# Sandwich transformer layer on 8 cores: five x buffers, a V projection that takes its first four tiles in step, and V weights held back

## The reference

```python
q = (x @ w_q.T).reshape(B, S, H, Hd)      # likewise k, v
scores = jnp.einsum('bqhd,bkhd->bhqk', q, k) * scale
p = jax.nn.softmax(scores, axis=-1)
o = jnp.einsum('bhqk,bkhd->bqhd', p, v).reshape(B, S, D)
attn = o @ w_o.T
ffn = (silu(x @ w_gate.T) * (x @ w_up.T)) @ w_down.T   # hidden 8192

x = x + _layernorm(attn(_layernorm(x)))
x = x + _layernorm(ffn(_layernorm(x)))
```

## Time and profile before

| What | Value |
|---|---|
| Time, median of 3 runs | 2342.87 us (2342.86 to 2342.87) |
| Profiled execution, its own time | 2356.09 us |
| Its span, slowest core (core 4) | 2354.5 us |
| Spans of cores 0 to 7 | 2334.1, 2336.4, 2339.5, 2337.5, 2354.5, 2354.4, 2333.1, 2339.7 us |
| Mean granted TensorE clock, cores 0 to 7 | 0.994, 0.993, 0.992, 0.992, 0.980, 0.980, 0.993, 0.991 |
| TensorE busy, core 4 | 2285.1 us, 97% of the span |
| ACT, DVE, POOL busy, core 4 | 584.7, 575.4, 130.8 us |
| Chain that ended last | PE 90%, DVE 3%, ACT 2%, DMA 2%, issue 2% |
| Matmul of 128x512, from start to start at full clock | 215 ns; at half clock about 427 ns |

### The profile page before, as it was taken

One profiled execution on the slowest core, in us unless ns is written; L12 is line 12 of the kernel. 1 busy time (PEld: TensorE's weight loads), 2 busy tenths in 40 slices (PEclk: granted clock), 3 DMA queues, 4 the chain that ended last, 5 costly groups with the idle time before them and its releaser, 6 DMA issues.

```text
span 2354.5 us, 26957 instructions; the slowest of 8 cores (2333.1 to 2354.5 us)
## 1 busy us (share of the span) xinstructions
PE 2285.1 (97%) x10656; PEld 1034.9 (44%) x10656; DVE 575.4 (24%) x771; ACT 584.7 (25%) x781; POOL 130.8 (6%) x249
## 2 busy tenths in 40 slices
PE   4999999999999989999999999999999999999997
PEld 2444444444444434444444444444444444444443
DVE  4510034554554565510110110011001100000005
ACT  2421166666666642220000000000000000000003
POOL 1000000000000000000000000000000000000000
PEclk9999999999999988889999999999999999999999
DMA  9530021322323053154444444444444474435473
GB/s 229 156 59 14 9 36 28 63 37 35 56 36 63 10 125 135 72 99 74 79 75 78 76 77 77 76 77 75 79 74 80 73 131 75 77 67 87 75 179 143
DMA packets 43852, 186.34 MB, mean 79 GB/s; under 512 B 4816, under 2 KB 4816, under 8 KB 37584
## 3 DMA queue, kind: packets, MB, share of 16 engines
q0 software_dynamic: 36816, 134.27, 34.5%
q1 hardware_dynamic: 6912, 50.33, 6.1%
HBM read 302.06 MB, written 16.78 MB: 135 GB/s over the span
## 4 chain that ended last, share of the span: by engine, by line
PE 90%; DVE 3%; ACT 2%; DMA 2%; issue 2%; DVEq 0%; POOL 0%; ACTq 0%; SPq 0%; POOLq 0%
PE ps L162 90%; DMA wvs<-wv 1%; DMA xs<-xb 1%; DVE x L789 1%; ACT tt L165 0%; ACT pt L165 0%; ACT qt L168 0%; DVE rec L441 0%; DVE st L557 0%; DVE st L583 0%; ACT x L165 0%; ACT pvc L168 0%; ACT sdv L165 0%; ACT ln3t L168 0%; DVE fs L771 0%
## 5 line engine op out<-in xcount | busy, mean ns | idle before, releaser
L162 PE MATMUL ps<-ln3t,we 128*128 128x512 bf16 x4096 | 893.0, 381 | 0.8 <-ACT ln3t L168 0.8
L162 PEld LDWEIGHTS ps<-ln3t,we 128*128 128x128 bf16 x4096 | 402.4, 98 | 488.8 <-issue 25.8
L162 PE MATMUL ps<-ln1t,w 128*128 128x512 bf16 x1536 | 370.7, 379 | 3.0 <-ACT qt L168 3.0
L165 ACT ACTIVATE pt<-ps,kon 128x1024 bf16<-128x1024 f32 x256 | 284.7, 1114 | 191.8 <-PE ps L162 191.5
L165 ACT ACTIVATE sil<-ps 128x512 f32<-128x512 f32 x128 | 76.4, 597 | 789.5 <-PE ps L162 789.4
L162 PE MATMUL ps<-wvs,ln1t 128*128 128x512 bf16 x1024 | 227.1, 383 | 6.0 <-DMA wvs<-wv 6.0
L162 PEld LDWEIGHTS ps<-ln1t,w 128*128 128x128 bf16 x1536 | 148.2, 98 | 189.5 <-issue 14.7
L162 PE MATMUL ps<-ring,ga 128*128 128x512 bf16 x1024 | 222.1, 379 | 1.4 <-DVE gb L670 1.0
L162 PE MATMUL ps<-ring,gb 128*128 128x512 bf16 x1024 | 221.7, 379 | 0.0
L162 PEld LDWEIGHTS ps<-wvs,ln1t 128*128 128x128 bf16 x1024 | 100.4, 99 | 125.8 <-issue 10.7
L162 PE MATMUL ps<-pt,vt 128*128 128x512 bf16 x512 | 153.7, 382 | 0.7 <-ACT pvc L168 0.7
(11 more groups left out here) (50 smaller groups left out, 853.0 us busy)
## 6 DMA issues: line engine op xcount, KB each, us to landing
we<-wg POOLq DMA_DIRECT2D x64, 512.0 KB, 6.0
we<-wu POOLq DMA_DIRECT2D x64, 512.0 KB, 6.0
ring<-wd POOLq DMA_DIRECT2D x64, 512.0 KB, 6.1
xs<-xb SPq DMA_DIRECT2D x16, 1024.0 KB, 8.9
wvs<-wv POOLq DMA_DIRECT2D x16, 512.0 KB, 15.3
w<-wq POOLq DMA_DIRECT2D x16, 512.0 KB, 5.1
w<-wk POOLq DMA_DIRECT2D x16, 512.0 KB, 5.2
wo<-wo POOLq DMA_DIRECT2D x4, 2048.0 KB, 16.1
```

The source lines that it names most:

```text
L162: return op("t", lambda e: e.matmul(dst, lhsT, rhs, start=start, stop=stop), ctr)
L165: return op("s", lambda e: e.activation(dst, src, fn, bias=bias, scale=scale), ctr)
```

## The change

Six parts:

1. `xs` has five buffers in place of three. Two of them lie in the part of `vt` that group 3 of V fills later. The load of tile `tc` now waits for the normalisation of tile `tc - 5`; five loads go out at once.
2. Group 1 of V's weights and the first three Q and K weight tiles no longer follow group 0 at once: group 1's four chunks wait, one each, until x tiles 7, 9, 11 and 13 have landed, and the Q and K tiles until x tile 15 has.
3. `v_proj` is split by chunk into `v_part(tc, g, c)` (four matmuls) and `v_out` (the copy to `vt`). The first four tiles take group 0 in step: after the transposition of tile `tc`, the tiles before it take chunk `tc - 1`, then tile `tc` takes chunks 0 to `tc - 1`; chunk 3 follows for all four, then their four copies.
4. From tile 4 on the order is `v_proj(k, 0)`, `x_transpose(k + 1)`, and the next `k`.
5. Group 1 is projected after all of group 0; before, its tiles 0 to 11 stood between the tiles of group 0.
6. `x_norm_behind(tc)` puts the statistics of one tile ahead of the normalisation of the tile before it, as the old loop did.

```diff
-    XS = at("xs", OT_O, 6144, F32)
+    XS = [at("xs%d" % i, o, 2048, F32) for i, o in enumerate(
+        (OT_O, OT_O + 8192, OT_O + 16384, VT_O + 49152, VT_O + 57344))]
...
     def x_load(tc):
-        if tc >= 3:
-            wt("y", xnorm[tc - 3])
-        x_in[tc] = dma("y", XS.r((tc % 3) * 2048, 2048), xb[tc * 128:(tc + 1) * 128, :], dX[tc % 3])
+        if tc >= 5:
+            wt("y", xnorm[tc - 5])
+        x_in[tc] = dma("y", XS[tc % 5].r(0, 2048), xb[tc * 128:(tc + 1) * 128, :], dX[tc % 5])
...
-    def wv_load(g):
+    def wv_load(g, after=(None, None, None, None)):
+
         for c in range(4):
             if g >= 2:
                 wt("g", v_pe[(NTC - 1, g - 2)])
+            wt("g", after[c])
             wv_in[(g, c)] = dma("g", WV.r((g % 2) * 8192 + c * 2048, 2048), wv[g, c, :, :], dWV[g % 2][c])
 
     v_pe = {}
     v_sb = {}
-    v_n = [0]
-
-    def v_proj(tc, g):
-        b = 4 + v_n[0] % 4
-        v_n[0] += 1
-        wt("t", lnt[tc], bank_free[b])
-        for kc in range(NKC):
-            if kc % 4 == 0:
-                wt("t", wv_in[(g, kc // 4)])
+    v_bank = {}
+
+    def v_part(tc, g, c):
+
+        if c == 0:
+            v_bank[(tc, g)] = 4 + len(v_bank) % 4
+            wt("t", lnt[tc], bank_free[v_bank[(tc, g)]])
+        b = v_bank[(tc, g)]
+        wt("t", wv_in[(g, c)])
+        for kc in range(4 * c, 4 * c + 4):
             tok = mm(PS.r(b * 512, 512), LN1T.r(kc * 2048 + tc * 128, 128),
                      WV.r((g % 2) * 8192 + kc * 512, 512), kc == 0, kc == NKC - 1,
                      tV if kc == NKC - 1 else None)
-        v_pe[(tc, g)] = tok
-        wt("s", tok)
+        if c == 3:
+            v_pe[(tc, g)] = tok
+
+    def v_out(tc, g):
+        b = v_bank[(tc, g)]
+        wt("s", v_pe[(tc, g)])
         bank_free[b] = v_sb[g] = copy_s(VT.r(g * 8192 + tc * 512, 512), PS.r(b * 512, 512), sV)
+
+    def v_proj(tc, g):
+        for c in range(4):
+            v_part(tc, g, c)
+        v_out(tc, g)
...
-    for tc in range(3):
+    def x_norm_behind(tc):
+
+        if tc < NTC:
+            x_stats(tc)
+        x_norm(tc - 1)
+        if tc + 4 < NTC:
+            x_load(tc + 4)
+
+    for tc in range(5):
         x_load(tc)
     wv_load(0)
-    wv_load(1)
+    x_stats(0)
+
+    for tc in range(4):
+        x_norm_behind(tc + 1)
+        x_transpose(tc)
+        if tc:
+            for t in range(tc):
+                v_part(t, 0, tc - 1)
+            for c in range(tc):
+                v_part(tc, 0, c)
+    x_norm_behind(5)
+    for t in range(4):
+        v_part(t, 0, 3)
+    for t in range(4):
+        v_out(t, 0)
+    x_transpose(4)
+    for k in range(4, NTC):
+        if k + 2 <= NTC:
+            x_norm_behind(k + 2)
+        v_proj(k, 0)
+        if k + 1 < NTC:
+            x_transpose(k + 1)
+    wv_load(1, [x_in[tc] for tc in (7, 9, 11, 13)])
+    wt("g", x_in[NTC - 1])
     for m in range(3):
         w_load(m)
-    x_stats(0)
-    x_stats(1)
-    x_norm(0)
-    x_transpose(0)
-    x_load(3)
-    x_stats(2)
-    x_norm(1)
-    for k in range(NTC):
-        if k + 4 < NTC:
-            x_load(k + 4)
-        if k + 3 < NTC:
-            x_stats(k + 3)
-        if k + 2 < NTC:
-            x_norm_later = k + 2
-        else:
-            x_norm_later = None
-        if k == 0:
-            x_transpose(1)
-        if x_norm_later is not None:
-            x_norm(x_norm_later)
-        v_proj(k, 0)
-        if k + 2 < NTC:
-            x_transpose(k + 2)
-        if k >= 4:
-            v_proj(k - 4, 1)
-    wv_load(2)
-    for tc in range(12, NTC):
-        v_proj(tc, 1)
-    wv_load(3)
-    for g in (2, 3):
+    for g in (1, 2, 3):
+        if g >= 2:
+            wv_load(g)
         for tc in range(NTC):
```

More of the change, by code:

```diff
@@ L185, in build_nc @@
     NEGSH = KON.r(1, 1)
-    dX = [C("dX%d" % i) for i in range(3)]
+    dX = [C("dX%d" % i) for i in range(5)]
     dWV = [[C("dWV%d%d" % (i, c)) for c in range(4)] for i in range(2)]
@@ L222, in x_stats @@
     def x_stats(tc):
-        p, sl = tc % 2, tc % 3
+        p, xs = tc % 2, XS[tc % 5]
         wt("v", x_in[tc], aggr.get(tc - 2))
         for c in range(4):
-            op("v", lambda e, c=c: e.bn_stats(ST.r(p * 24 + c * 6, 6), XS.r(sl * 2048 + c * 512, 512)), vB)
+            op("v", lambda e, c=c: e.bn_stats(ST.r(p * 24 + c * 6, 6), xs.r(c * 512, 512)), vB)
         aggr[tc] = row_aggr(p)
     def x_norm(tc):
-        p, sl = tc % 2, tc % 3
+        p, xs = tc % 2, XS[tc % 5]
         row_rstd(p, aggr[tc])
@@ L234, in x_norm @@
         xnorm[tc] = op("v", lambda e: e.tensor_scalar(
-            XN.r(p * 2048, 2048), XS.r(sl * 2048, 2048), MV.r(p * 2, 1), SDV.r(p * 2 + 1, 1),
+            XN.r(p * 2048, 2048), xs.r(0, 2048), MV.r(p * 2, 1), SDV.r(p * 2 + 1, 1),
             ALU.subtract, ALU.mult), vXN)
```

## The result

| | Before | Changed |
|---|---|---|
| Median of 7 runs | 2342.87 us | 2356.57 us |
| Median of the undisturbed runs (7 and 4) | 2342.87 us | 2355.9 us |
| Ratio, with its 95% interval | | 1.0056 [1.0044, 1.0068] |
| Spans of the profiled cores | 2333.1 to 2354.5 us | 2349.6 to 2353.8 us |
| First Q projection, mean of 8 cores | 278.1 us (276.7 to 282.1) | 293.0 us (291.5 to 294.2) |

The change makes the kernel slower by 0.56%, 13.0 us; forecast were 12.4 us, 2355.3 us. On all eight cores the loss sits in the first stage: its end is 11.7 to 16.9 us later, 14.9 in the mean. In some executions part of the chip is granted a lower clock, whatever the kernel; the ratios leave out only the clearly slow ones, the counts and ranges of runs in the experiments all of them.

The account below looks back on a forecast made before the run. TensorE, 97% busy, was bound early by waits for data. Stage end 46.2 + 77.0 + 165.6 = 288.8 against 277.33, +11.5; clock +1.7, other cores -0.8: +12.4 on 2342.87 gives 2355.3 us, 8-in-10 range 2348.5 to 2366.

Parts of the forecast that it names:

- x and weights in pairs of 6.6 us: First stage's loads: an x tile and a weight chunk land together every 6.6 us, x3 at 25.5, x4 at 32.1.
- The early part: Tiles 0 to 3: tile 4's transposition starts at 46.2 with 64 matmuls done, won by about 6 us.
- The exposed latency: Tiles 4 to 15: each projection waits for its own tile's copies, 6.42 us for 4.35, 24.8 us of new waiting.
- The clock: TensorE in the new waits of about 2.0 us: one fall to the lower clock per core, 1.7 us.
- Stages after it, DVE, DMA, POOL cost nothing: Later stages unchanged and TensorE-bound; in the loop DVE's 5.2 us and DMA's 4.3 us fit within 6.42 us.
- The other cores: Other cores stood about 1 us later than core 4 before the change, so 0.8 us was taken off.
- (d): First-stage loads: engines serve by order of issue, tile 4 at 41, 2344.4 us or faster, 2338.5; chance 0.14.
- (b): Tiles 4 to 15: the clock falls in about half of the tiles or more, 2365.5 us at seven falls; chance 0.20.
- (c): First-stage loads: five buffers bring x no sooner, x4 at 35.0, tile 4 at 49.5, 2358.6 us; chance 0.08.
- The supply rival: Tiles 4 to 15: x and VectorE cannot feed a tile sooner than every 6.5 us; no chance given.

Follow-up runs that it names:

- e6: Changed kernel with part 3 undone: tiles 0 to 3 transposed first, then projected one after the other; fastest run 2363.7 us, ratio 1.0111 to the kernel before.
- e7: Kernel before with part 1 alone: five x buffers, loads two tiles further ahead; fastest run 2335.3 us, ratio 0.9965 to the kernel before.
- e3: Changed kernel with eight wasted matmuls between transposition and projection of tiles 4 to 15; fastest run 2348.6 us, ratio 1.0039 to the kernel before.
- e4: Changed kernel, but each chunk's four matmuls wait only for their own quarter's copy; fastest run 2332.8 us, ratio 0.9982 to the kernel before.
- e1: Changed kernel, from tile 4 on the next tile's transposition ahead of each projection; fastest run 2335.0 us, ratio 1.0019 [0.9985, 1.0053] to the kernel before.
- e2: e1 with each tile's square root also ahead of the previous tile's copies on ScalarE; fastest run 2326.7 us, ratio 0.9945 to the kernel before.
- e10: e2 with each chunk's matmuls waiting only for their own quarter's copy; fastest run 2327.8 us, ratio 0.9939 to the kernel before.
- e9: e2 with the first weight chunk held until x1 landed and x5 until the third chunk; fastest run 2328.0 us, ratio 0.9937 to the kernel before.
- e8: e2 with part 2 undone, no weights held; fastest run 2339.3 us, ratio 0.9987 to the kernel before.
- e5: Changed kernel with part 2 undone, no weights held; fastest run 2356.1 us, ratio 1.0076 to the kernel before.

## Why the prediction was right

By its own steps, measured on the mean of the eight cores where nothing else is said.

- **x and weights in pairs of 6.6 us.** Right: x3 at 24.3, x4 at 30.3, x5 at 37.0 on core 0, against 25.5, 32.1, 38.7. The pairs took 6.1 to 6.7, and began 1 us earlier than on core 4 before. This term came out 1.4 us short: tile 4's transposition at 44.8, forecast 46.2. The early part was won, as stated; e6 puts the worth of the steps at 8 us, e7 that of the buffers at 4 against the trace of before, nearer 6 against its usual run (below).
- **The exposed latency.** Right in mechanism and near in size: 6.52 us against 6.42. The hand-over from ACT to TensorE, for which I had no row, is 0.26 (copies' end at 68.46, start at 68.72), just above the bounds of 0.09 to 0.25; the 0.15 put in is what it costs where TensorE waits for one semaphore (0.14 in e3 and e4), and here it waits for two. Over twelve tiles: +1.2 us. e1, e2 and e4 take this wait away in three ways, and each time the loss goes.
- **The clock.** The term that was most mis-sized: one fall per core, 1.7 us, was counted; there were 20 on eight cores, two or three each, 4.2 us. e3 shows that they come of the waits.
- **Stages after it, DVE, DMA, POOL cost nothing.** Borne out: no wait for `xn` after tile 3, Q and K weights there in time, 48 projections in 165.8 us (forecast 165.6).
- **The other cores.** The 0.8 us between core 4 and the mean (277.3, 278.1) was read from the trace of before itself; no run here tests it.

The sum: the stage's end was forecast at 288.8 + 1.7 = 290.5. The terms' errors, -1.4 + 1.2 + 2.5 + 0.2, make it 293.0. By the traces the shift is 14.9 us in the mean, 2.5 more than forecast, yet the time grew by 13.0 only. The runs on record show where the rest went: the trace of before was an early execution. Its six cores at full clock ended at 2336.7 us in the mean; in 47 undisturbed runs of that kernel on three chips the cores end at 2338.8, 2339.9 and 2339.2 us (means of 25, 15 and 7 runs). From the start of the Q projection to the end the cores need 2057.9 to 2060.1 us in the mean in every kernel here, before, changed and e1 to e10 alike, so most of the missing 2 to 3 us lie in the first stage: the usual Q start of before is near 280 (an estimate, since there is one trace of it: 2338.8 to 2339.9 less 2059.1, the mean of the twelve), and the usual shift near 13. That the forecast of the time came within 1 us is therefore in part luck: the sum was 2.5 us short, and the trace on which it stood began its Q projections some 2 us early. The mechanism does not hang on this. For the same reason every gain in Q start against the kernel before is about 2 us too small here; comparisons among the changed kernel and the experiments are not touched.

Two small slips of the prediction: with x4 at 35.0 its own steps put tile 4 at 49.1, not 49.5 (+2.9 in place of +3.3), and rival (d) turns to a gain before 39.5, not 39.3. Neither moves a chance.

The rivals: (b) had the right direction, with a fifth of the tiles in place of half. (c) falls with the landings. (d) falls with them too: by order of issue x4 would land near 21.8, and it landed at 30.3; e9, which forces something like its order, brings tile 4 forward by 2.1 us only. The supply rival, formed afterwards, falls with e1, e2 and e4 for the changed kernel, and holds in e8, once the latency is out of the way.

Why the change lost although its parts are sound: buffers (e7: -4.3 us), steps (e6: -8.0) and held weights (e8 against e2: -13.4) each pay, but part 4, the order inside the loop, and part 5, group 1 taken out of it, turned a latency that had been covered into 2.0 us of waiting twelve times, and held weights pay only where x is the limit. With a different order in the loop the same parts give 2327 to 2329 us. No run put group 1 back into the loop, so the share of part 5 alone is argued, not shown: e1, e2 and e4 show that the wait goes without it, e3 that work put into the wait costs nothing there.

## What to carry to other kernels

When filler work is moved out of a loop, ask what latencies it was covering; here the copies behind a transposition had stood a whole projection away. Read that latency from the trace of before, where it is hidden but recorded (transposition's start to last copy's end), add the hand-over, and multiply by the trips. Then fix the order first: put the producer one trip ahead, and no small operation of its chain (here the square root) behind the long ones of another tile; the held weights paid only then (e5: nothing, e8: 13.4 us). The steps of the first tiles, which lie ahead of the loop, paid in the slow order too (e6).

## What the runs showed of the hardware

- TensorE's clock fell in short, regular waits: 2.0 us of waiting every 6.5 us gave two or three projections of 5.3 us in twelve per core, and none with 1.7 us of the wait filled (e3) or with waits of 0.43 us (e4). Each fall cost 1.7 us.
- The hand-over from ACT's copy to the waiting matmul takes 0.26 us where TensorE has two semaphores to wait for (changed kernel: copies' end 68.46, the two wait instructions at 68.50 and 68.61, start 68.72) and 0.14 where it has one (e3: copies' end 67.49, wait at 67.53, start 67.63; in all 96 tiles of the eight cores; e4 the same behind the first copy). So a second wait costs about 0.11 us, even when what it waits for has long come.
